# Macaron block with latent attention, one core: when projections and turns use the one shared PSUM bank

## The reference, cut to what matters

```
x = x + 0.5 * ffn(layernorm(x))      # 8 gated experts (best 2) and a shared one
x = x + attn(layernorm(x))
x = x + 0.5 * ffn(layernorm(x))      # the same weights

attn(x): h = layernorm(x) * scale + bias
         c_q, c_kv = h @ w_down_q.T, h @ w_down_kv.T          # 128 wide: the latents
         q, k, v = c_q @ w_up_q.T, c_kv @ w_up_k.T, c_kv @ w_up_v.T     # 16 heads of 64
         q, k = rope(q), rope(k)
         out = softmax(q k.T / 8) v, heads side by side, @ w_out.T + x
```

## Time and profile before

| | |
|---|---|
| median of 3 runs | 4095.92 us (4093.1 to 4099.3) |
| the profiled execution, its time | 4098.04 us |
| the profiled execution, its span | 4096.1 us |
| TensorE busy | 3897.4 us, 95% |
| GpSimd, vector, scalar engine busy | 2932.8, 2849.5, 2536.2 us (72, 70, 62%) |
| mean granted clock of TensorE | 0.988 |

### The profile page before, as it was taken

The page is one execution under the profiler, slowest core; times in us unless marked ns, Lnnn a source line. Parts: engine busy times, 40 slices in busy tenths (PEclk is TensorE's granted clock), DMA queues, the critical chain, the costliest instruction groups (busy, mean ns, idle before and its releaser), DMA issues. The chain is left out here.

```text
span 4096.1 us, 65749 instructions
## 1 busy us (share of the span) xinstructions
PE 3897.4 (95%) x24908; PEld 2207.7 (54%) x24908; DVE 2849.5 (70%) x3796; ACT 2536.2 (62%) x3191; POOL 2932.8 (72%) x1632
## 2 busy tenths in 40 slices
PE   7999979999999999999999999999999999989999
PEld 6888834444444444444444444444444444478888
DVE  5656567777777776777778777767776777565563
ACT  4455446766766676667666766766676666645544
POOL 3444448878877897888788878878887888634443
PEclk9999989999999999999999999999999999999999
DMA  3233221111211221121122212211211121142331
GB/s 123 99 124 109 81 93 53 60 55 59 83 53 53 71 66 53 61 81 53 53 66 76 63 53 66 68 50 60 86 55 53 58 79 62 33 145 76 125 114 63
DMA packets 192772, 300.36 MB, mean 73 GB/s; under 512 B 50328, under 2 KB 100937, under 8 KB 191817
## 3 DMA queue, kind: packets, MB, share of 16 engines
q1 hardware_dynamic: 192456, 296.17, 22.3%
HBM read 201.20 MB, written 26.73 MB: 56 GB/s over the span
## 5 line engine op out<-in xcount | busy, mean ns | idle before, releaser
L1088 DVE TENSOR_REDUCE atNM<-atPS 128x2 f32<-128x1024 f32 x1024 | 1225.7, 1219 | 452.8 <-PE atPS L899 450.1
L1029 ACT ACTIVATE atPT<-atPS 128x1024 f32<-128x1024 f32 x1024 | 1014.0, 1024 | 773.1 <-PE atPS L920 766.7
L1187 POOL TENSOR_TENSOR atACC<-atACC,atPT 128x1024 f32<-128x1024 f32 x510 | 1238.7, 2429 | 89.3 <-ACT atPT L1029 39.1
L931 PE MATMUL atPO<-atPT,atV 128*64 128x512 f32 x4096 | 1014.2, 602 | 0.0
L1187 POOL TENSOR_TENSOR atACC<-atPT 128x1024 f32<-128x1024 f32 x255 | 606.6, 2379 | 262.8 <-PE atOT L953 181.7
L1020 ACT ACTIVATE atPS<-atSH 128x1024 f32<-128x1024 f32 x683 | 687.4, 1023 | 50.8 <-DVE atNM L1088 34.0
L920 PE MATMUL atPS<-atQH,atKL 64*128 64x512 f32 x2048 | 459.9, 445 | 66.3 <-DVE atPS L1094 51.7
L931 PEld LDWEIGHTS atPO<-atPT,atV 128*64 128x64 f32 x4096 | 259.0, 136 | 456.5 <-issue 433.1
L899 PE MATMUL atPS<-atKH,atQH 64*128 64x512 f32 x2048 | 444.0, 431 | 10.0 <-ACT atQH L1009 7.9
L1094 DVE COPY atPS<-atSH 128x1024 f32<-128x1024 f32 x341 | 418.7, 1228 | 37.9 <-DMA atSH<-atMD 11.4
L920 PE MATMUL atPS<-atQH,atKH 64*128 64x512 f32 x2048 | 406.6, 393 | 0.0
(11 more groups left out here) (278 smaller groups left out, 6461.5 us busy)
## 6 DMA issues: line engine op xcount, KB each, us to landing
atSH<-atMD SPq DMA_DIRECT2D x128, 512.0 KB, 4.3
atVT<-atR SPq DMA_DIRECT2D x508, 128.0 KB, 2.1
f1GB<-f1GD SPq DMA_DIRECT2D x128, 256.0 KB, 6.7
f2GB<-f2GD SPq DMA_DIRECT2D x128, 256.0 KB, 6.8
atRSUM<-atRD SPq DMA_DIRECT2D x126, 256.0 KB, 4.0
X<-x SPq DMA_DIRECT2D x4, 1024.0 KB, 6.0
XS<-x SPq DMA_DIRECT2D x16, 256.0 KB, 3.6
x<-X SPq DMA_DIRECT2D x16, 256.0 KB, 2.3
```

Source lines behind the costliest of these rows:

```text
L931: ins = pe.eng.matmul(PO[HI[h], :], V[n % 2][:, j, HI[h]], PT[k % NPT][:, h, :], start=j == 0, stop=j == T - 1)
L1029: act.eng.activation(PT[k % NPT][:, :, :], PS[ring.of[step]][:, :, :], ACT.Exp, scale=SCALE).then_inc(grown.sem)
L1088: dve.eng.tensor_reduce(NM[:, q // 4, :, q % 4, t], PS[ring.of[step]][:, :, :], AX.X, ALU.max, negate=True).then_inc(most_out.sem)
L1187: pool.eng.tensor_tensor(total[:, :, :], begun[:, :, :], PT[k % NPT][:, :, :], ALU.add).then_inc(gathered.sem)
```

## The change

It does three things to the list, and adds or removes no instruction.
- `TURNS` is changed in its last four entries: the last two turns of a batch come 4 periods (8 tiles) sooner, and the latents after them are placed one tick or one period otherwise.
- If the others of x have no user of `atOT` among them, the others of x+1 are taken into slot 1 as well, ahead of its attends.
- If slot 2 would begin with a `raise` and ends with another user of `atOT`, the `raise` is moved behind that one (`apart`).

```
-            TURNS = [(-21, late), (-20, late), (-17, early), (-17, late), (-9, early), (-9, late), (-8, early), (-8, late)]
+            TURNS = [(-21, late), (-20, late), (-17, early), (-17, late), (-13, late), (-12, late), (-9, late), (-8, late)]
...
+            def uses(steps):
+
+                return [s for s in steps if s[0] in ("turn", "latent", "raise", "value", "row", "sum", "outward")]
+
+            def apart(one, two):
+
+                raised = [s for s in one if s[0] == "raise"]
+                if raised and uses(two):
+                    return [s for s in one if s not in raised], two + raised
+                return one, two
...
                 order += tile("score", x) + most_of(x) + tile("fill", x + 2) + tile("score", x + 1)
-                order += others_of(x) + held + tile("attend", x - 1)
-                order += gathers(held + tile("attend", x - 1))
+                now, some, more = held + tile("attend", x - 1), others_of(x), []
+                if not uses(some):
+                    more = others_of(x + 1)
+                order += some + more + now + gathers(now)
                 order += most_of(x + 1) + tile("score", x + 2) + most_of(x + 2)
                 now, held = tile("attend", x), tile("attend", x + 1)
                 if x % T < T - 1:
                     now, held = now + held, []
-                order += tile("fill", x + 3) + others_of(x + 1) + tile("fill", x + 4) + now + gathers(now) + others_of(x + 2)
+                one, two = apart(others_of(x + 1), others_of(x + 2))
+                order += tile("fill", x + 3) + one + tile("fill", x + 4) + now + gathers(now) + two
```

## The result

| | before | after |
|---|---|---|
| median of 7 runs each, same chip | 4096.63 us (4093.10 to 4100.98) | 4111.86 us (4104.54 to 4115.66) |
| ratio, 95% interval | | 1.0035 (1.0023 to 1.0047) |
| the profiled execution, its time | 4098.04 us | 4114.02 us |
| its span | 4096.1 us | 4112.0 us |
| mean granted clock of TensorE | 0.988 | 0.983 |

The change costs 15 us. I had predicted 4097.7, no change that could be measured, in a range of 4079 to 4115 with a chance of 0.28 for slower. The range holds the result; the sign is not the one I thought likeliest.

What follows compares the result with a forecast made beforehand. TensorE, busy 95%, was taken as the bound, so gains lay in its waits. The terms +8.4 + 5.6 - 2.0 - 5.8 - 3.7 - 1.7 + 1 gave +1.8 us: 4097.7 in terms of the median, range 4079 to 4115.

Steps and rivals of the forecast that it cites:

- Position 3: Raise moved behind the sum waits for the sum's copy behind two scalar fills: 0.42 us slower, 20 times, +8.4.
- what the split gives back from position 0: Position 0's gain mostly lost at position 3, where the split of q still ends after the same gather: +5.8 us.
- Positions 7 and 9: Raise in slot 1 delays scalar fills by its evictions: +0.4 us 14 times (+5.6), and -0.15 13 times (-2.0).
- Positions 1 and 0: Slot 1 fillers remove the score's stall: -0.72 us 8 times (-5.8); -0.95 10 times (-9.5), -3.7 after the split.
- my terms for the rest: Positions 7, 9, 1 and 0, turns without raises behind them, and +1 us for a later DRAM chain at position 9.
- The terms of `apart`: Position 3 +8.4 us, raises behind turns +9.6, raises behind rows +4.6, less two waits that go.
- The turns: 14 waits behind an outward go, -12.7 us; 10 raises behind turns wait 0.96 longer, +9.6; with rows and others -1.7.
- the rows at position 9: In 4 places a raise comes right behind a row, behind the scalar fills: +1.15 us each, +4.6.
- A: Faster: vector engine not in the way, filled stalls stay filled; -28 us, 4068, half of it (4083) likelier; chance 0.3.
- B: Slower: at position 3 the split of q before the reductions takes 3.0 us, not 2.0; +20, 4117; chance 0.2.
- C: Slower: the late rotate, waiting for swap DMAs, pushes GpSimd's gathers beyond 6 us of slack; 4117 us; chance 0.07.
- D: At position 3 `apart` parts nothing, raise and sum stay neighbours in the other order; already in the sum.

Runs made afterwards that it cites:

- copy sooner: Kernel with new TURNS, no raise into slot 1 and `apart` only at sums, plus the sum's copy ahead of the second fill on the scalar engine: 4059.19 us.
- split later: The whole change, with the split of q behind the two reductions on the vector engine at position 3: 4088.62 us.
- the kernel that spares them: The whole change, with `apart` only where the user behind the raise is a sum: 4087.42 us.
- the fastest kernel: New TURNS, slot 1 taking others of x+1 without raises, `apart` at sums, sum's copy before the second fill, split of q behind the reductions: 4053.24 us.

## Why the prediction was right and wrong

**Position 3** was right: +0.42 for each group. Against the kernel before, eight of the twenty groups came out at +0.37 to +0.45, and the group above at 0.41 once its split is allowed for. The other twelve lie anywhere from -1.03 to +2.78, by the gathers that their splits meet and by the half clock. I had 8.4 for the order and 5.8 for what the split gives back from position 0, 14.2; the twenty measured 12.5, which with such a spread is in part luck. The expected wait, for the copy on the scalar engine and not for the vector engine, is the one that the trace names. With `apart` at sums as the only difference it was 9.75. The two edits at either end of the chain shorten that wait, from 36.2 to 22.3 us (copy sooner) and from 37.4 to 18.6 (split later), so that the chain is shown and not only read.

**Positions 7 and 9.** At 14 groups of position 7 it was +0.37 or +0.38 for my +0.4, with the stall of 1.3. Not in my sum: 0.19 in the group behind. Position 9 was -0.27 for -0.15, with +0.2 at position 12 behind it. (The -0.15 was set against the 0.77 of position 7; against the 0.70 that the earlier trace rows shows for position 9 it would have been -0.12.) Together my terms are too small by about 3 us, and the experiment without raises in slot 1 confirms the sign.

**Positions 1 and 0** were right in themselves (-0.72 for -0.72 at 8 groups, about -1.0 for -0.95 at 10). Seven more groups of position 1 won 0.94 each, since position 14's split on the scalar engine comes sooner, where I had put "nothing". But position 4 behind them gave 4.9 us back in all.

So the sum without `apart` was good, in part because misses of either sign cancelled in it (3 us too little at positions 7 and 9, some 2 too little gained at positions 1 and 4): my terms for the rest make -19.4 (5.6 - 2.0 - 5.8 - 3.7 - 12.7 - 3 + 1.2 + 1), and both parts without `apart` measured -20.5. The terms of `apart` make +21.2 (8.4 + 9.6 + 4.6 - 1.4), and it measured some 36.

**The turns are the step that failed.** I wrote: "In 10 places a raise now comes right behind a turn, whose eviction ends 1.47 us after its start (2361.90 to 2363.37): the raise waits until 1.55, not 0.59, +0.96 each". That row shows a turn whose scalar engine had been idle for 1.61 us before. In slot 2 the scalar engine first has its two fills:

```profile
1964.86 1.97 ACT L1034 ACTIVATE atPS<-atSH 128x1024 f32<-128x1024 f32 x2
1966.75 0.59 ACT L1050 ACTIVATE atAT<-atPO 128x512 f32<-128x512 f32 x1
1967.23 0.78 ACT L1010 ACTIVATE atHT<-atOT,lns 128x512 f32<-128x512 f32 x1
```

This turn started at 1965.07, and its raise at 1968.06: the eviction began 2.16 us after the turn, behind two fills and the copy of an attend's output. The raise waited 2.99 us and not 1.55, 2.4 more than the 0.59 of a free bank. It was so at all five places of position 7; at the five of position 5 it was 1.06 more, near my 0.96. I had worked out the same queue at position 3 and for the rows at position 9, and did not do it for the turns. Places behind a turn and a row cost 20.2 us against the kernel that spares them, for the 12.8 in my sum (9.6 and 4.6, less the 1.4 of two waits that go; the rows were right, 4.4 for 4.6).

**The clock is the step that was not there.** Nothing in my sum prices a pause of TensorE but by its own length. The changed kernel has 7 more stretches at 1.2 GHz between 600 and 3500 us than the one before. The seven groups compared above lost 8.1 us to theirs, 1.2 each, so by this estimate 7 stretches cost some 8 us. With some 6 to 7 of the turns (20.2 for 12.8, with perhaps 0.9 of half clock in the 20.2) that is some 15, and my sum was short by 13 (15.2 measured, 1.8 forecast). So the two steps account for the miss in size, but not to the microsecond: misses of either sign stand in the other terms, and what a stretch costs was read from seven groups of one profile.

**The rivals.** A (the vector engine is not in the way, faster) fails at position 7, where the predicted stall stands; what was true in it is that both first parts gain. B (a longer split in front of the reductions): it took a mean of 2.01 us at position 3 before and 2.09 after, nowhere near the 3.0 of that case, nor the 2.4 from which it decides. Over all positions, after and in the form of the earlier trace rows:

```profile
L1097 DVE TENSOR_TENSOR atQL<-atU,atQH x64: 1214/1520/3370, 547.6 to 3519.0; 128x1024 fp32r<-128x1024 f32 x64
```

It found the right engine and the wrong reason: the split is in the chain in both orders and costs no more than it did. What makes it expensive is that somebody now waits for the end of the chain. That it ends some 1.1 us after the gather it meets held again (in the group above, the first of two gathers runs from 2139.35 for some 2.4, and the split ends at 2142.81). C was tried, and the time did not fall with the wait. D was in the sum.

## What to carry to other kernels

A step that is moved behind another user of a shared buffer waits for that user's eviction, and the eviction's price is its place in its engine's queue, not its length: write out that queue at the new place each time, also where a row of the same step elsewhere shows a short one. Where such a wait appears, try first to move the eviction ahead of work that nobody needs yet, on its own engine: here that turned a loss of 9.8 us into a gain of 7.9, without a change of TensorE's order. And look at the granted clock behind every wait of some 2 us before pricing the wait by its length.

## What the runs showed of the hardware

TensorE's granted clock fell to 0.5, 1.2 GHz, for 3.4 us at a time (once 6.8 in the changed kernel) in a stage where it is otherwise 1.0 and TensorE is busy 96% (600 to 3500 us of the kernel before; all counts here are of this window). Nine of the ten stretches of the changed kernel begin in or within 1.3 us behind a wait of 1.9 us or more of TensorE, the tenth behind one of 1.82. There are 6 such waits before and 14 after; with `apart` alone 9, and in the fastest kernel 3. The stretches are 3, 10, 5 and 1. The kernel with `apart` at sums and no raise in slot 1 has 9 such waits and 8 stretches, and the same kernel without any `apart` 9 waits and 3 stretches. So more long waits go with more stretches, but not every long wait brings one, and the kernel with `apart` alone has fewer than its waits would let one think. What decides which wait brings one stays open here, and no run took the clock away alone, so that the 8 us are worked out from groups with and without a stretch and are not a measurement by themselves.

In such a stretch a row of two matmuls of a score took 0.63 us for 0.40, and the group it fell on lost 0.5 to 1.9 us against the same group in a kernel without it.

The split of q shows a second thing, which I had expected: its time goes with what GpSimd does. It took 1.21 to 1.22 us at its shortest and up to 3.37 with the same operands. Before the change 50 of the 64 splits began while a gather ran, after it 49, and each of them ended 1.08 to 1.21 us after that gather; all others took 1.22. The Trainium skill (SBUF — State Buffer, Who interferes with whom) says that a vector instruction with two SBUF inputs and a GpSimd instruction that reads SBUF exclude each other. The traces agree in both orders of the vector engine's work, so the remedy that the split later tried is not to make it faster but to put nothing urgent behind it.
